# Edge sort of a four-layer graph network: the running table carried per four tiles instead of two

## The chip, the cores and the metric

The kernel runs on one core of a Trainium2 chip. Five engines take part: PE (TensorE, matmuls, which write the banks of PSUM), DVE (VectorE), ACT (ScalarE), POOL (GpSimd, which here mainly issues indirect DMAs, one row address per partition) and SP (which only issues DMAs). Each runs its own list of instructions in order and waits on counting semaphores that the others raise. The metric is the device time of one execution in microseconds (us), lower is better.

## What is computed

Four message-passing layers over 3125 nodes and 103125 edges (100000 random ones and a self-loop each), all with 256 features. Each layer has a segment sum over one end of the edges:

```python
_o = jnp.argsort(dst, stable=True)
src = src[_o]; dst = dst[_o]
...
h = layernorm_relu(x)
x = x + _L0_gnn_ref(h, edge_index, edge_attr_18, ...)               # softmax and sums by src
x = x + _L1_gnn_ref(layernorm_relu(x), edge_attr_64, edge_weight, ...)  # by dst
x = x + _L2_gnn_ref(..., src, dst, edge_type_8)                     # by dst
x = x + _L3_gnn_ref(..., src, dst, ...)                             # by dst
```

The kernel first writes the edges' records (attributes and a few words) into two arrays in HBM, one ordered by `src` and one by `dst`, so that the layers find the edges of a node block next to each other. The change is in this counting sort alone, in the two passes that scatter the records.

## The kernel before

`sort_all` (from line 152) does the sort. A tile is 128 edges, one per partition; there are 808 tiles. A key is split into `hi` (one of 25 node blocks) and `lo` (the place in the block). The position of an edge in the order is a start for its key, plus the number of edges with the same key in earlier tiles, plus the number of them ahead of it in its own tile.

- The **running table** (25 x 128, one entry for each key) holds the start plus what earlier tiles added. It is accumulated in PSUM bank `TABLE` by one matmul per tile, one-hot `hot_hi` by one-hot `hot_lo` (line 700), and copied by ACT into the SBUF tile `table` (line 604), which has two buffers.
- The **lookup** (line 705) multiplies the turned one-hots `hot_hi_t` with `table`, in fp32, into bank 2 or 3 (`c % 2`); DVE then picks the column by a product with `hot_lo` and a sum, which gives `base` (line 649). Two lookup banks are used in turn: the lookup of tile c waits on `row_used` for tile c-2's base.
- The **rank** (line 641) compares an edge's key with the keys of the tile, laid out along the free axis in bank 4 or 5 by `keys` (line 684), and sums the matches under the mask `earlier`.
- `positions` (line 631) adds base and rank for two tiles; POOL waits for it (`pos_ready`) and issues two indirect DMAs, one per tile, each of 128 record rows (line 564).

Tiles go in **steps** of G = 8, 101 of them per pass: first `scatter(keys_of[0], ...)` with `FirstPass` beside it (by `src`), then `scatter(keys_of[1], ...)` with `SecondPass` (by `dst`). A hardware loop holds `ROUND` = 4 steps; the order inside a step is written out by hand for each engine. DVE: ranks of tiles 0-3; bases 0, 1; one-hots of the next step (lines 340, 342); base 2, positions of the first pair; base 3, positions of the second pair; ranks of tiles 4-7; bases 4, 5; base 6, positions of the third pair; base 7, positions of the fourth; then what runs beside (in the first pass the one-hots for the next histogram). PE, for each pair d = 0 to 3 of the step: wait for `table_ready`, two table matmuls, two lookups; behind pair 1 it turns the first half of the next step's one-hots (line 672), behind pair 2 it turns the second half and lays out the first keys, behind pair 3 it lays out the second keys and does the histogram matmuls. ACT, for each pair: wait for `table_moved` and `looked_up`, copy the table; keys, turned one-hots (line 583) and the record's words (line 591) lie between. Records and `pos_i` have four buffers (`ROUND`), the one-hots, `base` and `rank` two.

Of the kernel before, what the change touches and what calls it, by code (L numbers as in the profile page):

```python
# [6 lines left out]
BF16 = mybir.dt.bfloat16  # L7
# [5 lines left out]
P = 128  # L13
# [12 lines left out]
PAIRS = G // 2  # L26
BUFS, BUFS2 = 4, 6
# [124 lines left out]
def sort_all(nc, C, A, x, by_src, by_dst, projected, kv0, q0):  # L152
# [48 lines left out]
    with phase(nc, "sort") as ph:  # L201
# [29 lines left out]
        junk = ph.sbuf("junk", [P, G, 3 * P], BF16)  # L231
        earlier = ph.sbuf("earlier", [P, 2, P], BF16)
# [42 lines left out]
        with ph.block() as block:  # L275
# [34 lines left out]
            def _(dve):  # L310
                dve.tensor_copy(ps[:, IOTA, 0:P], C.iota[:])
                dve.tensor_scalar(ident_hi[:], C.ident_b[:], float(BN), None, ALU.mult)
                dve.memset(earlier[:, 0, :], 1.0)
                dve.tensor_copy(earlier[:, 1, :], C.lower[:])
# [196 lines left out]
        def scatter(K, attr_dram, words, beside):  # L511
# [22 lines left out]
            with ph.block() as block:  # L534
# [36 lines left out]
                def _(act):  # L571
# [27 lines left out]
                    def body(j, b, ahead, tail):  # L599
                        n = at(j, b)  # L600
                        for d in range(PAIRS):
                            act.wait_ge(table_moved, n(PAIRS, d + 1))
                            act.wait_ge(looked_up, n(G, 2 * d))
                            act.copy(table[0:NB, (d + 1) % 2, :], ps[0:NB, TABLE, 0:P]).then_inc(table_ready, 1)  # L604
                            if ahead and d == 0:
                                if not opening(j, b, 1):
                                    act.wait_ge(pos_ready, n(PAIRS, 0))
                                keys(*ahead)
                            if ahead and d in (1, 2):
                                turn(*ahead, d - 1)  # L610
                            beside.scalar(act, j, b, d, tail)
# [6 lines left out]
                def _(dve):  # L618
# [14 lines left out]
                    def body(j, b, ahead, tail):  # L633
                        n, u = at(j, b), b % 2
                        for h in range(2):
                            dve.wait_ge(keys_ready, n(2, h + 1))
                            for c in range(4 * h, 4 * h + 4):

                                first, mates = (0, P) if c % 2 else (1, 0)
                                end = P * (c % 4) + P  # L640
                                last = dve.scalar_tensor_tensor(out=junk[:, c, 0:P + mates].rearrange("p (t e) -> p t e", e=P),  # L641
                                                                in0=ps[:, 4 + h, end - P - mates:end].rearrange("p (t e) -> p t e", e=P),
                                                                scalar=key_cur[:, u, c:c + 1], in1=earlier[:, first:2, :],
                                                                op0=ALU.is_equal, op1=ALU.mult, accum_out=rank[:, u, c:c + 1])
                            last.then_inc(ranked, 1)
                            for c in range(4 * h, 4 * h + 4):
                                dve.wait_ge(looked_up, n(G, c + 1))

                                dve.scalar_tensor_tensor(out=junk[:, c, 2 * P:3 * P], in0=ps[:, 2 + c % 2, 0:P], scalar=1.0,  # L649
# [11 lines left out]
                def _(pe):  # L661
# [2420 lines left out]
```

## Time and profile before

| | |
|---|---|
| time, median of 3 runs | 10085.68 us (10085.18 to 10108.67) |
| span of the profiled execution, first to last instruction | 9823.2 us |
| time that lies outside the span | 10085.7 - 9823.2 = 262.5 us |
| first scatter pass, first to last scatter | 267.9 to 1592.1 us, 1324.2 us |
| second scatter pass | 1620.6 to 2913.6 us, 1293.0 us |
| POOL busy in the first pass / DVE / PE | 784.5 / 799.9 / 762.9 us of 1329 |

The profile is one execution. It gives busy times per engine and line, what ended the idle time ahead of an instruction (the releaser), and a timeline. A releaser is found from the semaphores: "<-DVE sort_pos_i L631" is a wait that this line's end released; "<-remote" means that the semaphore rose just before, but no instruction's recorded end lies near that moment; "<-issue" means that no semaphore rose then. The ends of matmuls are modelled. All times below are from this execution's span, and the 262.5 us outside it are taken as unchanged.

### The profile page before, as it was taken

What the parts mean: (1) busy time and instruction counts of PE and PEld (TensorE: products, weight loads), DVE (VectorE), ACT (ScalarE), POOL (GpSimd) and SP (SyncE); (2) the same over time, 40 slices, a digit from 0 to 9 for tenths busy, and PEclk for the clock granted to TensorE, in tenths of its full rate; (3) what the DMA queues carried; (4) which work ended last, traced back from release to release, by engine and by line L of the source; (5) the groups of instructions that cost most, each with busy time, mean ns of one, the idle gap of its engine ahead of it and who ended that gap; (6) DMA issues with size and microseconds to landing.
All of it is one profiled execution on the core that took longest, in us unless ns stands there. A gap on an engine that the chain in (4) does not pass through costs nothing. (4 is left out here: it accounts for less than half of the span.)

```text
span 9823.2 us, 140985 instructions
## 1 busy us (share of the span) xinstructions
PE 6503.9 (66%) x32549; PEld 4804.2 (49%) x32550; DVE 5122.6 (52%) x15163; ACT 3750.0 (38%) x11176; POOL 5197.7 (53%) x5192
## 2 busy tenths in 40 slices
PE   8555555666657777777588888879644445566664
PEld 7445544554444555555366666656433324344443
DVE  6556655555545555555587777841122223344445
ACT  3212212222225555555266666734100001566663
POOL 0555655665655545455166666620466663566664
PEclk9776666666668988899799999989766667677776
DMA  7301102111114444344265565632333333333333
GB/s 221 92 13 14 13 13 61 27 26 27 26 27 110 107 104 107 98 108 103 91 172 159 157 161 156 166 102 69 84 89 89 92 90 70 84 90 89 89 89 75
DMA packets 1039015, 873.73 MB, mean 89 GB/s; under 512 B 746842, under 2 KB 855410, under 8 KB 1038360
## 3 DMA queue, kind: packets, MB, share of 16 engines
q0 software_dynamic: 259600, 655.15, 25.1%
q1 hardware_dynamic: 723939, 158.04, 8.3%
q10 hardware_dynamic: 54948, 54.63, 1.7%
q8 instruction: 196, 3.21, 0.1%
q14 instruction: 332, 2.71, 0.1%
HBM read 733.27 MB, written 134.17 MB: 88 GB/s over the span
## 5 line engine op out<-in xcount | busy, mean ns | idle before, releaser
L1164 POOL DMA_INDIRECT edges_kv<-kv,edges_rec x1712 | 1832.2, 1070 | 1432.6 <-issue 713.7
L1274 PE MATMUL banks<-edges_kv,edges_hot 128*128 128x288 f32 (+2 forms) x5136 | 1715.8, 489 | 757.7 <-DVE edges_kv L1549 621.1
L1274 PEld LDWEIGHTS banks<-edges_kv,edges_hot 128*128 128x128 f32 x5136 | 1158.9, 236 | 1138.0 <-ACT edges_pair_sums L1426 337.2
L564 POOL DMA_INDIRECT by_src_records<-sort_by_src_rec,sort_pos_i x808 | 784.5, 971 | 774.2 <-issue 483.2
L705 PE MATMUL banks<-sort_table,sort_hot_hi_t 128*128 128x128 f32 x3232 | 880.6, 413 | 423.9 <-DVE sort_junk L649 244.2
L1722 POOL DMA_INDIRECT edges_rows<-rel,edges_rec x856 | 811.5, 948 | 583.2 <-DMA edges_rec<-by_dst_records 326.3
L1164 POOL DMA_INDIRECT edges_kv<-feat,edges_rec x856 | 826.3, 965 | 526.1 <-issue 331.7
L564 POOL DMA_INDIRECT by_dst_records<-sort_by_dst_rec,sort_pos_i x808 | 784.6, 971 | 536.9 <-DVE sort_pos_i L631 302.2
L1738 PE MATMUL banks<-edges_rows,edges_hot 128*128 128x256 f32 x1712 | 604.2, 500 | 694.9 <-issue 417.8
L649 DVE SCALAR_TENSOR_TENSOR sort_junk<-banks,sort_hot_lo 128x128 bf16<-128x128 f32 x1616 | 438.5, 286 | 1055.8 <-remote 755.5
L705 PEld LDWEIGHTS banks<-sort_table,sort_hot_hi_t 128*128 128x128 f32 x3232 | 687.9, 291 | 508.2 <-DVE sort_junk L649 289.9
L1738 PEld LDWEIGHTS banks<-edges_rows,edges_hot 128*128 128x128 f32 x1712 | 416.4, 251 | 883.1 <-issue 583.1
L1391 ACT ACTIVATE edges_off<-columns,edges_column 128x128 bf16<-128x128 f32 x2568 | 784.5, 390 | 0.0
L583 ACT COPY sort_hot_hi_t<-banks 25x512 f32<-25x512 f32 x404 | 232.4, 575 | 1404.2 <-remote 780.0
L1776 DVE TENSOR_TENSOR agg<-banks,agg 128x256 f32 x428 | 181.0, 423 | 928.4 <-DMA tables_far<-far 606.1
L1363 ACT ACTIVATE edges_apart<-banks,minus_p 128x512 bf16<-128x512 f32 x642 | 431.5, 691 | 571.8 <-DMA sort_feat<-in_edge_attr_dram 311.7
L700 PE MATMUL banks<-sort_hot_lo,sort_hot_hi 128*128 128x128 bf16 x1616 | 299.9, 282 | 488.1 <-ACT sort_table L604 482.2
L641 DVE SCALAR_TENSOR_TENSOR sort_junk<-banks,sort_key_cur,sort_earlier 128x128 bf16<-128x128 f32 x1616 | 576.7, 413 | 5.8 <-PE banks L684 5.8
L1567 DVE TENSOR_TENSOR edges_kv<-banks,edges_kv 128x256 f32<-128x256 f32 x428 | 179.5, 420 | 687.7 <-PE banks L1234 393.6
L1234 PE MATMUL banks<-x,edges_hot_t 128*128 x1712 | 494.8, 414 | 58.3 <-issue 42.2
L1549 DVE TENSOR_TENSOR edges_kv<-edges_kv 128x1024 f32<-128x1024 f32 x428 | 519.9, 1215 | 3.4 <-ACT edges_kv L1408 3.4
L1582 DVE TENSOR_TENSOR edges_kv<-banks,edges_kv 128x256 f32<-128x256 f32 (+1 forms) x856 | 445.9, 552 | 137.5 <-remote 53.7
(440 smaller groups left out, 12977.2 us busy)
## 6 DMA issues: line engine op xcount, KB each, us to landing
edges_kv<-kv,edges_rec POOLq DMA_INDIRECT x1712
sort_feat<-in_edge_attr_dram SPq DMA_DIRECT2D x100, 256.0 KB
rel<-tables_stage SPq DMA_DIRECT2D x100, 252.0 KB
by_dst_records<-by_dst_blank ACTq DMA_DIRECT2D x1, 17120.0 KB
edges_rec<-by_dst_records SPq DMA_DIRECT2D x26, 640.0 KB
edges_rows<-rel,edges_rec POOLq DMA_INDIRECT x856
edges_kv<-feat,edges_rec POOLq DMA_INDIRECT x856
by_src_records<-sort_by_src_rec,sort_pos_i POOLq DMA_INDIRECT x808
```

Of the source, the lines that this page charges most:

```text
L564: pool.indirect_dma_start(O.rec, bass.IndirectOffsetOnAxis(ap=pos_i[:, b, c:c + 1], axis=0), rec[:, b, c, :], None).then_inc(scattered[b], 16)
L641: last = dve.scalar_tensor_tensor(out=junk[:, c, 0:P + mates].rearrange("p (t e) -> p t e", e=P), in0=ps[:, 4 + h, end - P - mates:end].re ...
L649: dve.scalar_tensor_tensor(out=junk[:, c, 2 * P:3 * P], in0=ps[:, 2 + c % 2, 0:P], scalar=1.0, in1=hot_lo[:, u, c, :], op0=ALU.mult, op1=A ...
L705: pe.matmul(ps[:, 2 + c % 2, 0:P], hot_hi_t[:, u, c, :], table[:, d % 2, :], start=True, stop=True).then_inc(looked_up, 1)
L1164: pool.indirect_dma_start(kv[:, r, c, 0:koff + DIM], None, tab, bass.IndirectOffsetOnAxis(ap=reci[:, b, c, idx:idx + 1], axis=0)).then_inc ...
L1234: last = pe.matmul(out[:, c, 2 * P - QW:2 * P], hot_t[:, b % 2, 2 * m + c, :], rows, start=(kind == 1), stop=(kind == 1 or c == 1), skip_g ...
L1274: last = pe.matmul(ps[:, 6 + m % 2, 0:OW], hot[:, b % 2, c, :], kv[:, b % BUFS, c, koff:koff + OW], start=(c % 2 == 0), stop=(kind != 1 an ...
L1391: last = act.activation(off[:, c, :], C.columns[:, c % 2, :], ACT.Abs, bias=column[:, b % 2, c:c + 1], scale=-1.0)
L1549: dve.tensor_tensor(v4, v4, bc(exps, dh), ALU.mult).then_inc(msg_done, 1)
L1582: dve.tensor_tensor(k2, by, k2, ALU.mult).then_inc(edges_used, 1)
L1722: pool.indirect_dma_start(rows[:, b, c, :], None, tab, bass.IndirectOffsetOnAxis(ap=reci[:, b, c, idx:idx + 1], axis=0)).then_inc(gathered ...
L1738: last = pe.matmul(sum_of(b, m), hot[:, b % SETS, c, :], rows[:, b, c, :], start=(c % 2 == 0), stop=(c % 2 == 1))
```

## The change

A step is now two groups of four tiles (`QUADS` = G // 4) instead of four pairs, in the table's hand-over between PE and ACT. Four table matmuls run in a row, then four lookups, with one copy of the table per four tiles. Since the table no longer tells of the tiles of the same four, a tile's rank counts those: tile c of four is compared with c + 1 tiles' keys (128, 256, 384, 512 columns), where it was 128 or 256. Positions and scatters stay in pairs. The work that lay behind pairs 1 and 2 or 2 and 3 on PE and ACT now lies behind the first and the second four.

```diff
-        junk = ph.sbuf("junk", [P, G, 3 * P], BF16)
-        earlier = ph.sbuf("earlier", [P, 2, P], BF16)
+        rank_junk = ph.sbuf("rank_junk", [P, QUADS, 10, P], BF16)
+        base_junk = ph.sbuf("base_junk", [P, G, P], BF16)
+        earlier = ph.sbuf("earlier", [P, 4, P], BF16)
...
-                dve.memset(earlier[:, 0, :], 1.0)
-                dve.tensor_copy(earlier[:, 1, :], C.lower[:])
+                dve.memset(earlier[:, 0:3, :], 1.0)
+                dve.tensor_copy(earlier[:, 3, :], C.lower[:])
...
-                        for d in range(PAIRS):
-                            act.wait_ge(table_moved, n(PAIRS, d + 1))
-                            act.wait_ge(looked_up, n(G, 2 * d))
-                            act.copy(table[0:NB, (d + 1) % 2, :], ps[0:NB, TABLE, 0:P]).then_inc(table_ready, 1)
-                            if ahead and d == 0:
+                        for q in range(QUADS):
+                            act.wait_ge(table_moved, n(QUADS, q + 1))
+                            act.wait_ge(looked_up, n(G, 4 * q))
+                            act.copy(table[0:NB, (q + 1) % 2, :], ps[0:NB, TABLE, 0:P]).then_inc(table_ready, 1)
+                            if ahead and q == 0:
...
-                            if ahead and d in (1, 2):
-                                turn(*ahead, d - 1)
-                            beside.scalar(act, j, b, d, tail)
+                            if ahead:
+                                turn(*ahead, q)
+                            beside.scalar(act, j, b, q, tail)
...
-                                first, mates = (0, P) if c % 2 else (1, 0)
-                                end = P * (c % 4) + P
...
+                                tiles = c % 4 + 1
+                                first = tiles * (tiles - 1) // 2
+                                last = dve.scalar_tensor_tensor(out=rank_junk[:, h, first:first + tiles, :],
+                                                                in0=ps[:, 4 + h, 0:tiles * P].rearrange("p (t e) -> p t e", e=P),
+                                                                scalar=key_cur[:, u, c:c + 1], in1=earlier[:, 4 - tiles:4, :],
...
-                        for d in range(PAIRS):
-                            pe.wait_ge(table_ready, n(PAIRS, d + 1))
-                            beside.tensor_table(pe, j, b, d, tail)
-                            for c in (2 * d, 2 * d + 1):
+                        for q in range(QUADS):
+                            quad = range(4 * q, 4 * q + 4)
+                            pe.wait_ge(table_ready, n(QUADS, q + 1))
+                            for c in quad:
                                 last = pe.matmul(ps[:, TABLE, 0:P], hot_hi[:, u, c, :], hot_lo[:, u, c, :],
                                                  start=False, stop=False, skip_group_check=True)
                             last.then_inc(table_moved, 1)
-                            for c in (2 * d, 2 * d + 1):
+                            for c in quad:
                                 pe.wait_ge(row_used[c % 2], n(4, c // 2))
-                                pe.matmul(ps[:, 2 + c % 2, 0:P], hot_hi_t[:, u, c, :], table[:, d % 2, :],
+                                pe.matmul(ps[:, 2 + c % 2, 0:P], hot_hi_t[:, u, c, :], table[:, q, :],
                                           start=True, stop=True).then_inc(looked_up, 1)
-                            if ahead and d in (1, 2):
-                                turn(*ahead, d - 1)
-                            if ahead and d in (2, 3):
-                                keys(*ahead, d - 2)
-                            beside.tensor(pe, j, b, d, tail)
+                            if ahead:
+                                turn(*ahead, q)
+                                keys(*ahead, q)
+                            beside.tensor(pe, j, b, q, tail)
```

In `FirstPass` and `SecondPass` the hooks follow: what hung on pair 3 hangs on the second four, what hung on pairs 0 and 1 on the first four, and the projection's matmuls (line 879), which stood behind pair 2, stand behind the second four.

PE in the middle of a step of the first pass, before: turning the first half (L672), the table and the lookups of tiles 4 and 5 (L700, L705), turning the second half.

```order
L672 MATMUL banks<-ident_b,sort_hot_hi 128x128 [waits sort_by_src_turned_copied,sort_by_src_hot_ready]
L672 MATMUL banks<-ident_b,sort_hot_hi 128x128 x3
L697 REGISTER_ALU
L700 MATMUL banks<-sort_hot_lo,sort_hot_hi 128x128 [waits sort_by_src_table_ready]
L700 MATMUL banks<-sort_hot_lo,sort_hot_hi 128x128
L705 MATMUL banks<-sort_table,sort_hot_hi_t 128x128 [waits sort_by_src_row_used0]
L705 MATMUL banks<-sort_table,sort_hot_hi_t 128x128 [waits sort_by_src_row_used1]
L670 REGISTER_ALU [waits sort_by_src_hot_ready]
L672 MATMUL banks<-ident_b,sort_hot_hi 128x128 [waits sort_by_src_turned_copied]
L672 MATMUL banks<-ident_b,sort_hot_hi 128x128 x3
```

The same place after (L674 turns, L686 lays out keys, L702 is the table, L707 the lookups of tiles 4, 5, 6, 7):

```order
L674 MATMUL banks<-ident_b,sort_hot_hi 128x128 [waits sort_by_src_turned_copied,sort_by_src_hot_ready]
L674 MATMUL banks<-ident_b,sort_hot_hi 128x128 x3
L680 REGISTER_ALU
L686 MATMUL banks<-sort_ident_hi,sort_halves 128x128 [waits sort_by_src_ranked,sort_by_src_seg_ready]
...
L702 MATMUL banks<-sort_hot_lo,sort_hot_hi 128x128 [waits sort_by_src_table_ready]
L702 MATMUL banks<-sort_hot_lo,sort_hot_hi 128x128 x3
L706 REGISTER_ALU
L707 MATMUL banks<-sort_table,sort_hot_hi_t 128x128 [waits sort_by_src_row_used0]
L707 MATMUL banks<-sort_table,sort_hot_hi_t 128x128 [waits sort_by_src_row_used1]
```

The eight key matmuls and all four table matmuls of tiles 4 to 7 now stand ahead of the lookups of tiles 4 and 5; the second turning and the first keys, which stood ahead of the lookups of tiles 6 and 7, do not any more.

DVE at the start of a step of the first pass, before:

```order
L641 SCALAR_TENSOR_TENSOR sort_junk,sort_rank<-banks,sort_key_cur,sort_earlier 128x128 [waits sort_by_src_keys_ready]
L641 SCALAR_TENSOR_TENSOR sort_junk,sort_rank<-banks,sort_key_cur,sort_earlier 128x256
L641 SCALAR_TENSOR_TENSOR sort_junk,sort_rank<-banks,sort_key_cur,sort_earlier 128x128
L641 SCALAR_TENSOR_TENSOR sort_junk,sort_rank<-banks,sort_key_cur,sort_earlier 128x256
L647 REGISTER_ALU
L649 SCALAR_TENSOR_TENSOR sort_junk,sort_base<-banks,sort_hot_lo 128x128 [waits sort_by_src_looked_up]
```

And after:

```order
L643 SCALAR_TENSOR_TENSOR sort_rank_junk,sort_rank<-banks,sort_key_cur,sort_earlier 128x128 [waits sort_by_src_keys_ready]
L643 SCALAR_TENSOR_TENSOR sort_rank_junk,sort_rank<-banks,sort_key_cur,sort_earlier 128x256
L643 SCALAR_TENSOR_TENSOR sort_rank_junk,sort_rank<-banks,sort_key_cur,sort_earlier 128x384
L643 SCALAR_TENSOR_TENSOR sort_rank_junk,sort_rank<-banks,sort_key_cur,sort_earlier 128x512
L649 REGISTER_ALU
L651 SCALAR_TENSOR_TENSOR sort_base_junk,sort_base<-banks,sort_hot_lo 128x128 [waits sort_by_src_looked_up]
```

Nothing moves on DVE; the third and fourth rank of a half grow by 256 columns each.

## Rows read from the trace of the kernel before

**Rows 1.** The page: span, and busy time of each engine in it.

```profile
span 9823.2 us, 140985 instructions
...
PE 6503.9 (66%) x32549; PEld 4804.2 (49%) x32550; DVE 5122.6 (52%) x15163; ACT 3750.0 (38%) x11176; POOL 5197.7 (53%) x5192
```

**Rows 2.** Busy time and mean clock in the two scatter passes, windows view.

```profile
core 0: us, PE busy (x) PEld busy (x) DVE busy (x) ACT busy (x) POOL busy (x), PEclk, DMA share, GB/s
266.00:1595.00 1329.00, 762.94 (x5618) 650.46 (x5615) 799.86 (x4021) 274.41 (x1199) 784.50 (x808) 0.68 0.14 27
1620.00:2916.00 1296.00, 811.22 (x4952) 641.39 (x4950) 700.57 (x3985) 308.39 (x1473) 784.56 (x808) 0.65 0.12 26
```

**Rows 3.** Line 564, the scatters: duration min/median/max in ns, first and last start.

```profile
L564 POOL DMA_INDIRECT by_src_records<-sort_by_src_rec,sort_pos_i x808: 966/972/1168, 267.9 to 1592.1; - x162
L564 POOL DMA_INDIRECT by_dst_records<-sort_by_dst_rec,sort_pos_i x808: 966/972/988, 1620.6 to 2913.6; - x162
```

**Rows 4.** Waits of 300 to 1600 us: total us, times, longest.

```profile
DVE sort_junk L649 <- remote: 384.3, 116, 4.9
ACT sort_table L604 <- remote: 315.5, 92, 8.9
...
POOL by_src_records L564 <- DVE sort_pos_i L631: 284.8, 98, 4.8
```

**Rows 5.** Timeline of one step of the first pass: start, us, engine, work, [idle before <-releaser].

```profile
1500.30 0.29 DVE L649 SCALAR_TENSOR_TENSOR sort_junk<-banks,sort_hot_lo 128x128 bf16<-128x128 f32 x1 [4.55 <-remote]
...
1501.48 0.97 POOL L564 DMA_INDIRECT by_src_records<-sort_by_src_rec,sort_pos_i  x1 [2.42 <-DVE sort_pos_i L631]
...
1502.76 0.97 POOL L564 DMA_INDIRECT by_src_records<-sort_by_src_rec,sort_pos_i  x1 [0.30 <-issue]
...
1505.91 0.15 DVE L631 TENSOR_TENSOR sort_pos_i<-sort_base,sort_rank 128x2 int32<-128x2 f32 x1
...
1506.45 1.17 PE L705 MATMUL banks<-sort_table,sort_hot_hi_t 128*128 128x128 f32 x4
...
1506.88 0.97 POOL L564 DMA_INDIRECT by_src_records<-sort_by_src_rec,sort_pos_i  x1 [0.60 <-issue]
...
1507.41 0.63 PE L672 MATMUL banks<-ident_b,sort_hot_hi 128*128 128x128 bf16 x4
...
1507.86 0.29 DVE L649 SCALAR_TENSOR_TENSOR sort_junk<-banks,sort_hot_lo 128x128 bf16<-128x128 f32 x1
...
1508.90 0.90 PE L705 MATMUL banks<-sort_table,sort_hot_hi_t 128*128 128x128 f32 x4
...
1510.05 0.57 ACT L583 COPY sort_hot_hi_t<-banks 25x512 f32<-25x512 f32 x1 [2.84 <-remote]
...
1510.71 0.97 POOL L564 DMA_INDIRECT by_src_records<-sort_by_src_rec,sort_pos_i  x1 [0.31 <-issue]
1513.03 0.29 DVE L649 SCALAR_TENSOR_TENSOR sort_junk<-banks,sort_hot_lo 128x128 bf16<-128x128 f32 x1 [4.67 <-remote]
1513.06 0.26 ACT L604 COPY sort_table<-banks 25x128 f32<-25x128 f32 x1 [2.44 <-remote]
...
1514.22 0.97 POOL L564 DMA_INDIRECT by_src_records<-sort_by_src_rec,sort_pos_i  x1 [2.54 <-DVE sort_pos_i L631]
```

**Rows 6.** Line 641 by shape, both passes: busy us, mean ns | idle before.

```profile
L641 DVE SCALAR_TENSOR_TENSOR sort_junk<-banks,sort_key_cur,sort_earlier 128x256 bf16<-128x256 f32 x806 | 385.8, 479 | 0.0
L641 DVE SCALAR_TENSOR_TENSOR sort_junk<-banks,sort_key_cur,sort_earlier 128x128 bf16<-128x128 f32 x806 | 279.2, 346 | 2.9 <-PE banks L684 2.9
```

**Rows 7.** Timeline of a step of the second pass, same columns.

```profile
2500.55 0.29 DVE L649 SCALAR_TENSOR_TENSOR sort_junk<-banks,sort_hot_lo 128x128 bf16<-128x128 f32 x1 [2.56 <-PE banks L705]
...
2502.19 0.29 DVE L649 SCALAR_TENSOR_TENSOR sort_junk<-banks,sort_hot_lo 128x128 bf16<-128x128 f32 x1 [1.34 <-PE banks L705]
...
2507.31 0.16 DVE L631 TENSOR_TENSOR sort_pos_i<-sort_base,sort_rank 128x2 int32<-128x2 f32 x1
...
2508.48 0.97 POOL L564 DMA_INDIRECT by_dst_records<-sort_by_dst_rec,sort_pos_i  x1 [0.30 <-issue]
```

More of the change, by code:

```diff
@@ L26 @@
 PAIRS = G // 2
+QUADS = G // 4
 BUFS, BUFS2 = 4, 6
@@ L647, in body @@
                                 dve.wait_ge(looked_up, n(G, c + 1))
-                                dve.scalar_tensor_tensor(out=junk[:, c, 2 * P:3 * P], in0=ps[:, 2 + c % 2, 0:P], scalar=1.0,
+                                dve.scalar_tensor_tensor(out=base_junk[:, c, :], in0=ps[:, 2 + c % 2, 0:P], scalar=1.0,
                                                          in1=hot_lo[:, u, c, :], op0=ALU.mult, op1=ALU.mult,
@@ L749, in count, with tensor @@
                 return last
-            @staticmethod
-            def tensor_table(pe, j, b, d, tail):
-                pass
             @classmethod
-            def tensor(cls, pe, j, b, d, tail):
-                if d == PAIRS - 1 and not opening(j, b, 1):
+            def tensor(cls, pe, j, b, q, tail):
+                if q == QUADS - 1 and not opening(j, b, 1):
                     pe.wait_ge(next_ready, at(j, b)(2, 0))
@@ L772, in scalar @@
             @staticmethod
-            def scalar(act, j, b, d, tail):
+            def scalar(act, j, b, q, tail):
                 pass
@@ L862, in tensor_table, with tensor @@
             @staticmethod
-            def tensor_table(pe, j, b, d, tail):
-                pass
-            @staticmethod
-            def tensor(pe, j, b, d, tail):
+            def tensor(pe, j, b, q, tail):
                 if tail or b != 2:
                     return
-                if d == 0:
+                if q == 0:
                     pe.wait_ge(cur_ready, j + 1)
@@ L875, in tensor @@
                     last.then_inc(cur_turned, 1)
-                if d == 2:
+                if q == 1:
                     pe.wait_ge(cur_copied, j + 1)
@@ L890, in scalar @@
             @staticmethod
-            def scalar(act, j, b, d, tail):
+            def scalar(act, j, b, q, tail):
                 if tail:
                     return
-                if b == 0 and d == 3:
+                if b == 0 and q == 1:
                     act.wait_ge(moments_ready, j * 3 + 3)
                     act.activation(root[:, 1:2], root[:, 0:1], ACT.Sqrt).then_inc(root_done, 1)
-                if b == 1 and d == 3:
+                if b == 1 and q == 1:
                     act.wait_ge(shift_ready, j * 2 + 2)
@@ L900, in scalar @@
                                    bias=shift[:], scale=root[:, 2:3]).then_inc(cur_ready, 1)
-                if b == 2 and d == 1:
+                if b == 2 and q == 0:
                     act.wait_ge(cur_turned, j + 1)
```

3 lines of the change are left out of this document (removed).

## The prediction, made before the changed kernel ran

> **What bounds the kernel now.** The page first: no engine fills the span, and the averages belong to many stages [rows 1]. The change touches only the two scatter passes, so I cut those out. In both, POOL, DVE and PE are each busy about 60% of the time [rows 2]: none is full, and the question is who waits for whom.
>
> POOL's own line shows the floor. A scatter takes 0.972 us and never much else [rows 3]; two in a row start 1.275 us apart (0.97 and an idle 0.30 that nothing ends) [rows 5]. A pass has 808, so its first and last would start 807 x 1.275 = 1029 us apart if POOL never waited. They start 1324.2 and 1293.0 us apart [rows 3]: POOL waits 295 and 264 us, 559 us together. That is all that this change could ever give. Nearly all of it is in one row: POOL waiting for the positions of line 631, 98 times in 101 steps, 2.9 us each [rows 4].
>
> Why are the positions late? One step answers it [rows 5]. DVE's base of tile 6 starts at 1500.30, and twelve and a half us later, at 1513.03, it is there again, after 4.67 us of idling on the lookup. But PE's record of that lookup (with tile 7's) is the one at 1508.90, which ends at 1509.80. ACT's table copy, which waits for an earlier matmul, starts within 0.03 us of DVE; both are put down to "remote", a semaphore that rose with nobody's end near it. So PE's results are there and are told late. When are they told? POOL's last scatter before it starves starts at 1510.71 and ends at 1511.68; the late signals come 1.35 us after that, and in the same way before 1500.30. Matmuls whose records end before about 1507.6 are seen at once (the lookups of tiles 4 and 5, 1506.45, are used at 1507.86); from the turning at 1507.41 on they are not. I read this as: while POOL has been issuing scatters for six or so us, PE's signals are held, and the bulk of them is let go when POOL has run dry. The cycle that follows is 8 scatters x 1.275 = 10.2, plus 1.35 until the held signals are seen, plus 1.19 from DVE's base at 1513.03 to POOL's start at 1514.22: 12.74 us, which is what a step takes (1293.0 / 101 = 12.8; the first pass, with some irregular stretches, 13.1).
>
> **The change part by part.**
>
> *Table hand-overs.* Two ACT copies of 0.26 us and two trips PE to ACT to PE fall out of each step. In the cycle above they are not late: at 1513 the copy and the base are released together, and POOL waits for the base. I value this at nothing; its cover is POOL's run of 10.2 us. What it is worth if that reading is wrong is a rival.
>
> The row shows two waits that end together, and gives no price for one signal more or less. The Trainium skill ("TensorE: Matmul & The Clock Gate", The cost: per-tile semaphore tail) says that increments by matmuls on completion serialize, at 26.3 ns each. By it the two increments fewer per step would save 202 x 2 x 0.026 = 11 us, against nothing in my sum.
>
> *Wider ranks.* 128 columns more cost 479 - 346 = 133 ns [rows 6]. Each half gains four times 128 columns, 0.53 us; a step 1.06 us, both passes 215 us of DVE. DVE in the first pass goes from 800 to 907 of 1329 us, still the smaller part, so it is not the total but the place that counts. In the first pass the first pair's positions start at 1505.91 and end at 1506.06; POOL's scatter for them starts at 1506.88, after 0.60 us of idling instead of 0.30 [rows 5]. From the end of positions to POOL's start always lie about 0.8 us (1514.22 has it too). So these positions are already 0.30 us late, nothing hides more, and the 0.53 us of the first half's ranks, which stand ahead of them, come on top of each step: 101 x 0.53 = 54 us. The second half's 0.53 us lies in front of base 4, while POOL works through four scatters (5.1 us from 1506.88); hidden. In the second pass the same positions end at 2507.47 for a scatter at 2508.48, 1.01 us; less the 0.82 it needs that leaves 0.19 us [rows 7]. That step holds the layer norm's statistics, as one in four does; there 0.34 us stick out, 25 x 0.34 = 9 us. The other steps have some 0.9 us more and hide it.
>
> *PE's order.* The lookups of tiles 4 and 5 now stand behind the first keys and two more table matmuls. From the two turnings and what lies between them to the next lookups [rows 5] I estimate 1.1 us for that; with the ranks' 0.53 they would start at about 1508.1 instead of 1506.45 and yield the first result near 1508.9. DVE asks for base 4 at 1507.86 + 1.06 = 1508.92. Just in time, if the signal is told at once: nothing. In return, nothing stands between lookups 5 and 6 any more; with the drain as the releaser that gives nothing either.
>
> *SBUF, DMAs:* the same scatters, loads and stores; no cost.
>
> Sum: 54 + 9 = 63 us on 10085.7, 10149 us. Bounds: below, the whole wait of POOL, -559; above, the restart of the second rival.
>
> **The rivals.**
>
> *Slower by a longer restart.* With the first result at 1508.9, lookup 4 falls 7.4 us into POOL's run that began at 1501.48, where the trace shows signals held. Then after the drain DVE must do base 4, PE lookup 6, DVE base 6, before positions can go. The second pass shows such a hop: base at 2500.55, the next but one base on the same bank at 2502.19, 1.64 us [rows 7]; unheld it would be nearer 1.2. If it hits each step of the first pass only: 101 x 1.64 + 63 = 229, 10315 us; both passes, less what the second already pays: up to +350. It decides from the point where lookup 4 ends later than six or so us into the run. I take 10330.
>
> *Faster: fewer signals ahead of the needed one.* Not all held signals wait for the drain: ACT's copy at 1510.05 was let go alone, 3 us before the rest [rows 5]. Before, three signals of PE (the turning, the keys, the table) stand ahead of lookup 6; now none does. If held signals leave one by one, lookup 6 takes the early slot, positions come up to 3 us sooner and POOL's 2.5 us gap closes. ACT's 315.5 us of table waits [rows 4], too, would halve. In half the steps of both passes: 0.5 x 202 x 2.5 = 252, less 63: -190, 9895 us; in a fifth of them -40. Against it: lookups 4 to 7 also come later.
>
> *No difference.* The first pass' irregular stretches (13.1 against 12.8 a step, 30 us) go while the ranks cost their 54, or DVE's late pair is absorbed in the wait behind it: within 30 us of before. This is also how it would look if the hand-over simply weren't where time goes and the ranks had cover that one step doesn't show.
>
> **How the numbers follow.** A measurement can tell about 0.3%, 30 us. Forecast (10149; by itself 10105 to 10200): 0.40, of which 0.07 lies inside 30 us. Longer restart: 0.17. No difference: 0.18. Faster: 0.25. So slower 0.33 + 0.17 = 0.50, same 0.25, faster 0.25. For the range I leave out the part of the faster case below 9950 (0.09) and of the restart case above 10350 (0.08): 9950 to 10350.
>
> **What would show it.** The ranks at 346, 479, about 612 and 745 ns. POOL's scatters still in runs of eight with one wait of about 2.5 us a step ahead of the third pair, and a second, of 0.8 us instead of 0.3, ahead of the first pair in the first pass; the passes at about 1378 and 1302 us from first to last scatter. A wait of 3.7 us or more in front of the third pair, with base 4 released together with ACT's table copy, is the longer restart. POOL runs longer than eight scatters, or table waits of ACT that vanish along with POOL's, are the faster case. It is wrong at its root if PE's signals are told at once in the new order: then POOL's floor, not the drain, would set the step.

## The result: 1.6 to 2.0% slower, and the profile after

The changed kernel took 10250.5 us (median of 4; 10245.3 to 10280.0), the kernel before 10085.4 (median of 4). Three of those four are the runs of the table above, from before the prediction; the one that was added is 10056.7 us. The medians give 1.0164, 165 us. The reported ratio is 1.0196, with a 95% interval of 1.0164 to 1.0228, which by its size goes with the added run (10250.5 / 10056.7 = 1.0193). So the loss is 165 to 197 us, its size rests on few runs of before, and the changed kernel was measured again further down. The forecast was 10149 us, slower by 63. The sign and the range held; the size was 2.6 to 3.1 times too small.

The time of the profiled execution is its span and 1.7 us (10246.5 against 10244.8), and so it is in every later run of both kernels. So nothing to speak of stands outside the span. By that rule the execution of [rows 1], with a span of 9823.2 us, took about 9825 us and was shorter than its neighbours; this is worked out, its own time is not on record. The two profiles differ by 421.6 us, of which some 256 belong to that one execution of before. A second trace of before, further down, is the one to compare with.

The scatters of the changed kernel, in the view of one line (duration min/median/max in ns, first and last start), which answer to [rows 3]:

```profile
L566 POOL DMA_INDIRECT by_src_records<-sort_by_src_rec,sort_pos_i x808: 964/970/1167, 266.6 to 1748.4; - x162
L566 POOL DMA_INDIRECT by_dst_records<-sort_by_dst_rec,sort_pos_i x808: 964/970/982, 1776.3 to 3236.3; - x162
```

A scatter costs what it did, 0.97 us. The passes take 1481.8 and 1460.0 us from first to last start, where 1378 and 1302 were forecast. The waits of 300 to 1700 us (total us, times, longest) answer to [rows 4]:

```profile
ACT sort_table L606 <- remote: 705.7, 95, 8.0
...
POOL by_src_records L566 <- DVE sort_pos_i L633: 457.4, 108, 5.0
DVE sort_base_junk L651 <- remote: 448.8, 95, 5.4
```

The wait for the positions is still about one a step, but it is longer: 457.4 us in 108 times, 4.2 us each, where it was 2.9. Where it stands is in the timeline of a step (start, us, engine, work, [idle before <-releaser]), which answers to [rows 5]:

```profile
1502.64 0.97 POOL L566 DMA_INDIRECT by_src_records<-sort_by_src_rec,sort_pos_i  x1 [4.83 <-DVE sort_pos_i L633]
...
1506.44 0.40 PE L702 MATMUL banks<-sort_hot_lo,sort_hot_hi 128*128 128x128 bf16 x4
...
1511.56 0.97 POOL L566 DMA_INDIRECT by_src_records<-sort_by_src_rec,sort_pos_i  x1 [0.30 <-issue]
1514.29 0.26 ACT L606 COPY sort_table<-banks 25x128 f32<-25x128 f32 x1 [7.86 <-remote]
1514.34 0.29 DVE L651 SCALAR_TENSOR_TENSOR sort_base_junk<-banks,sort_hot_lo 128x128 bf16<-128x128 f32 x1 [5.00 <-remote]
...
1514.55 0.29 DVE L651 SCALAR_TENSOR_TENSOR sort_base_junk<-banks,sort_hot_lo 128x128 bf16<-128x128 f32 x1
...
1514.76 0.36 DVE L342 TENSOR_TENSOR sort_hot_hi<-banks,sort_by_src_hi 128x200 bf16<-128x200 f32 x1
1515.04 1.22 DVE L344 TENSOR_TENSOR sort_hot_lo<-banks,sort_by_src_lo 128x1024 bf16<-128x1024 f32 x1
1516.17 0.28 DVE L651 SCALAR_TENSOR_TENSOR sort_base_junk<-banks,sort_hot_lo 128x128 bf16<-128x128 f32 x1
...
1516.38 0.16 DVE L633 TENSOR_TENSOR sort_pos_i<-sort_base,sort_rank 128x2 int32<-128x2 f32 x1
...
1517.36 0.97 POOL L566 DMA_INDIRECT by_src_records<-sort_by_src_rec,sort_pos_i  x1 [4.83 <-DVE sort_pos_i L633]
```

POOL's scatter at 1502.64 is the first of a step, and so the wait now stands ahead of the first pair, not the third. The eight scatters run to 1512.53. PE's table matmuls of 1506.44 end at 1506.84, but ACT's copy that waits for them starts at 1514.29. Then DVE does base 0, base 1, the two one-hot instructions of the next step (1514.76 to 1516.17, 1.41 us) and base 2, and only at 1516.38 the first positions. That is the restart: 1.8 us until the signals are told, 2.0 from there to the positions, 0.16 for them and 0.8 to POOL's start at 1517.36, 4.8 us, of which 0.30 stand between any two scatters. The cycle is 10.2 + 4.5 = 14.7 us, and the starts of every eighth scatter are 14.7 us apart (median, first pass; 14.6 in the second). In [rows 5] the same instructions stood outside the restart, and the cycle was 12.8.

### The profile page after: what moved, and what is told of

It reads as the page before. It is cut to its first block and busy times, and to the rows that moved or that the text cites. A ratio compares the mean times of both kernels' runs of the same rounds, so it can differ in the third digit from the quotient of the medians.

```text
span 10244.8 us, 139889 instructions
## 1 busy us (share of the span) xinstructions
PE 6397.7 (62%) x32549; PEld 4750.4 (46%) x32550; DVE 5365.0 (52%) x15163; ACT 3678.7 (36%) x10772; POOL 5181.8 (51%) x5192
## 5 line engine op out<-in xcount | busy, mean ns | idle before, releaser
L707 PE MATMUL banks<-sort_table,sort_hot_hi_t 128*128 128x128 f32 x3232 | 817.8, 395 | 1372.2 <-DVE sort_base_junk L651 1312.7
L707 PEld LDWEIGHTS banks<-sort_table,sort_hot_hi_t 128*128 128x128 f32 x3232 | 642.6, 277 | 1472.2 <-DVE sort_base_junk L651 1409.9
L651 DVE SCALAR_TENSOR_TENSOR sort_base_junk<-banks,sort_hot_lo 128x128 bf16<-128x128 f32 x1616 | 446.5, 288 | 1142.5 <-remote 994.6
L643 DVE SCALAR_TENSOR_TENSOR sort_rank_junk<-banks,sort_key_cur,sort_earlier 128x128 bf16<-128x128 f32 (+1 forms) x1616 | 792.8, 547 | 5.8 <-PE banks L686 5.8
L606 ACT COPY sort_table<-banks 25x128 f32<-25x128 f32 x404 | 103.1, 255 | 1470.7 <-remote 1325.9
```

The costliest lines, as they stand in the source:

```text
L643: last = dve.scalar_tensor_tensor(out=rank_junk[:, h, first:first + tiles, :], in0=ps[:, 4 + h, 0:tiles * P].rearrange("p (t e) -> p t e", ...
L651: dve.scalar_tensor_tensor(out=base_junk[:, c, :], in0=ps[:, 2 + c % 2, 0:P], scalar=1.0, in1=hot_lo[:, u, c, :], op0=ALU.mult, op1=ALU.mu ...
L707: pe.matmul(ps[:, 2 + c % 2, 0:P], hot_hi_t[:, u, c, :], table[:, q, :], start=True, stop=True).then_inc(looked_up, 1)
```

## The experiments

The kernels of a group below ran on the same chip, each group on another one. The groups fall into two kinds: in two of them the kernel before took about 10,070 us, as at first, in three about 8,290 us. I call the kinds A and B. Each of these five chips was used in one group only, so whether the kind belongs to the chip or to the time of the runs isn't shown. What the profiles show of the difference is under the last heading. Times are compared within a group.

### Before, again; and its rank widths, the one-hots and PE's order apart (kind B)

The kernel before, unchanged.

> The kernel before, unchanged, to have its time and trace from the same chip as the experiments. The changed kernel's time was its span + 1.7 us, while the profiled execution of before had a span of 9823.2 us against a median of 10085 us. Theory D (that execution was an unusually short one; the time is always span + about 2 us): the span here is about 10083 us, the two scatter passes take about 2880 us together (1424 and 1393 in scatters) instead of 2617, some 14.0 us a step instead of 12.8, and the changed kernel's real loss is 0.8 us a step. Rival F (a fixed part outside the span): span 9823 us again, time 262 us above it.

It took 8287.2 us, ratio 1.0002 (0.9992 to 1.0011) to its twin. The profiled execution took 8282.5 us with a span of 8280.8; rival F falls here, but theory D's numbers can't be tried where no signal comes late. The scatters:

```profile
L564 POOL DMA_INDIRECT by_src_records<-sort_by_src_rec,sort_pos_i x808: 965/969/1166, 266.4 to 1294.5; - x162
L564 POOL DMA_INDIRECT by_dst_records<-sort_by_dst_rec,sort_pos_i x808: 965/969/986, 1316.6 to 2344.0; - x162
```

1028.1 and 1027.4 us: the floor of 1029 us that the prediction worked out, with no waits above it. The same 0.97 us a scatter, the same program; and in the whole list of waits of this trace no row has "remote" as its releaser. Here is what POOL waits for between 300 and 1200 us:

```profile
POOL by_src_records L564 <- issue: 202.5, 663, 0.8
...
POOL by_src_records L564 <- DVE sort_pos_i L631: 13.4, 44, 0.3
```

These are the 0.30 us between two scatters (215.9 us in 707 times), whoever they are put down to. Now the wide ranks in the kernel before (shortened):

```
-  in0=ps[:, 4 + h, end - P - mates:end], in1=earlier[:, first:2, :]
+  in0=ps[:, 4 + h, 0:tiles * P],         in1=earlier[:, mask:mask + tiles, :]
   # tiles = c % 4 + 1; masks: zero for the earlier pair, then as before
```

> The kernel before with only the changed kernel's rank widths (128, 256, 384 and 512 columns, masks that are zero for the earlier pair, so the same results). The change's extra rank time is 2 x (133 + 266) = 0.8 us a step on DVE. Theory R (the late second pair of each four is the loss): ratio to before 1.010 to 1.016, 100 to 165 us, and a wait that grows by about 0.8 us a step. Theory C (the loss comes from where the eight scatters' row is cut and what DVE and ACT must redo before it starts again): ratio 0.999 to 1.006.

8296.3 us, ratio 1.0008 (0.9998 to 1.0017). Theory C had named 0.999 to 1.006, but on kind B POOL's issue covers everything, so it says only that the wider ranks have cover where nothing is told late. They are 1.06 us a step, as in the prediction, and not the 0.8 us of the expectation: the third and the fourth rank of a half grow by 133 + 133 ns each (613 and 746 ns against 346 and 479). In the changed kernel, the one-hots moved:

```
-  if c == 1 and ahead:      # the next step's one-hots, line 656
+  if c == 3 and ahead:
```

> The changed kernel with the next step's one-hots (two DVE instructions, 1.41 us) issued behind the positions of the second pair instead of behind base 1, so that they no longer stand between the first lookups and the first pair of positions. Theory C: the wait ahead of the first pair falls from 4.5 to about 3.1 us, a step takes 13.3 us instead of 14.7, and the time is 10250 - 202 x 1.4 = 9967 us (ratio to before 0.988). Theory R: the ranks are what is late, the time stays within 40 us of 10250 (ratio 1.012 to 1.020).

8426.9 us, 1.0173 (1.0156 to 1.0190): slower than either kernel is here. The passes took 1136.0 and 1040.3 us: the steps of the first are 11.2 us long. Neither expectation could be tried, since both were for kind A. I read the loss so: PE turns the one-hots, ACT copies them, PE looks up with them; each of these starts later by what the one-hots were put back, and the loop over the engines is then longer than 10.2 us. That reading is argued, no run splits it. And PE's order of before in the changed kernel:

```
-  if ahead:
-      turn(*ahead, q)
-      keys(*ahead, q)       # both behind each four lookups
+  if ahead and c in (3, 5): # inside the loop over the tiles, behind lookup c
+      turn(*ahead, c // 4)
+  if ahead and c in (5, 7):
+      keys(*ahead, c // 2 - 2)
```

> The changed kernel (table per four tiles, wide ranks) with the next step's turns and key copies standing between PE's lookups as in the kernel before: the turn of half 0 behind lookup 3, turn 1 and keys 0 behind lookup 5, keys 1 behind lookup 7, instead of behind each four. Theory P (PE's order alone made the loss: keys and turns stand ahead of lookups): the cut goes back to the third pair and the time to 10085 +- 30 us (ratio 1.000). Theory C says that order only shifts which signals are told late: between 10190 and 10300 us (ratio 1.010 to 1.021). Theory R: 10250 as well.

8302.3 us, 1.0016 (1.0006 to 1.0025), with POOL at its floor as above. It decides nothing, since the changed kernel wasn't beside it and no step has a cut.

### The changed kernel again, and lookups in one bank per four (kind A)

> The changed kernel, unchanged. In the last four runs the kernel before took 8288 us instead of 10085, its POOL ran one scatter per 1.273 us through both passes without a wait (10.18 us a step), and no engine waited for a signal without a releaser; so these runs lack what makes the steps 12.8 to 14.7 us long in the first traces. Theory C (the change only moves the place where signals that come late cut the row of eight; where none come late, POOL's issue covers everything): if the kernel before takes 8288 us again, ratio 0.999 to 1.004; if it takes about 10085 us, 1.016 again. Rival L (the changed kernel's own loop over DVE, ACT and PE, with four table moves behind each other and the one-hots ahead of the first pair, is longer than 10.18 us): ratio 1.008 to 1.017 at 8288 us, with a wait ahead of the first or third pair in each step of the first pass, as with the one-hots later (10.2 to 11.2 us a step).

This group had the kernel before at 10069.3 us, and the changed kernel at 10236.3: ratio 1.0151 (1.0102 to 1.0201), passes of 1475.5 and 1455.6 us. The first result repeats in sign and rough size. The second kernel (shortened):

```
-  pe.wait_ge(row_used[c % 2], n(4, c // 2))          # for each lookup
-  pe.matmul(ps[:, 2 + c % 2, 0:P], ...).then_inc(looked_up, 1)
+  # once per four: the bank's last readers of the step before
+  last = pe.matmul(ps[:, 2 + q, P * (c % 4):P * (c % 4) + P], ...)
+  ...
+  last.then_inc(looked_up, 1)                        # once per four
```

> The changed kernel with the four lookups of a four written into one bank's four quarters, told by one signal, and PE waiting once per four for the bank's last reader of the step before, instead of for each lookup's predecessor by two. Theory C where signals come late: fewer round trips behind the late signal, but lookups 4 to 7 can also run ahead of it: the cut stays ahead of the first pair, 0.3 to 0.8 us a step less than the changed kernel (60 to 160 us). Where none come late: nothing, within 0.3% of the changed kernel. Rival L: PE's lookups were in its loop, at 8288 us it is faster than the changed kernel by 0.5 to 1%.

10222.3 us, 14 us below the changed kernel, whose interval covers that; the passes, 1482.0 and 1483.4 us, are not shorter. Three fewer signals a four and no lookup that waits for its predecessor by two: it buys nothing that these runs can tell, and the wait stays ahead of the first pair in nearly every step. The 60 to 160 us that I expected did not come. The likely reason, from the step shown above, is that the first signal that DVE needs is already a held one, and the restart begins with it; no run tries this.

### PE's order, the one-hots and the changed kernel once more (kind B)

> The same kernel as in the run of e4 (the changed kernel with PE's turns and key copies between the lookups, as before). There the kernel before took 8288 us and nothing came late; the last call had the kernel before at 10069 us and the changed one at 1.015. If the kernel before takes about 10070 us in this call too: theory P (the change loses because its PE order sends the turns and keys ahead of nothing, so that the row of eight is cut ahead of the first pair instead of the third) expects a ratio of 0.996 to 1.004 and the wait back ahead of the third pair; theory R (wide ranks) and theory M (the table moved per four) expect 1.012 to 1.018 and the wait of 4.5 us ahead of the first pair. If the kernel before takes 8288 us: 1.0016 again, which decides nothing.

Kind B: 8301.5 us, 1.0013 (1.0003 to 1.0022), which decides nothing, as said.

> The same kernel as in the run of e3 (the changed kernel, the next step's two one-hots behind the second pair's positions). If the kernel before takes about 10070 us in this call: theory C (when signals come late, DVE's 1.41 us of one-hots stand in the restart between base 1 and base 2) expects the wait ahead of the first pair to fall from 4.5 to 3.1 us and a ratio of 0.985 to 0.995; rival L (the one-hots delay PE's turns for the next step, which is what cost 1.6% where nothing came late) expects 1.015 to 1.035, later turns giving back more than the restart gains. If the kernel before takes 8288 us: 1.017 again.

8417.4 us, 1.0149 (1.0132 to 1.0166). Here the changed kernel ran beside it:

> The changed kernel beside the two above. With the kernel before at about 10070 us: 1.015 again (10220 to 10255 us). With the kernel before at 8288 us, not yet measured: theory C expects 0.999 to 1.004, since the loss is then no property of the change but of late signals; rival L expects 1.008 to 1.017 and waits ahead of the first pair.

8300.8 us, ratio 1.0011 (1.0001 to 1.0020). **On kind B the change costs nothing in the passes**:

```profile
L566 POOL DMA_INDIRECT by_src_records<-sort_by_src_rec,sort_pos_i x808: 965/970/1167, 268.2 to 1296.5; - x162
L566 POOL DMA_INDIRECT by_dst_records<-sort_by_dst_rec,sort_pos_i x808: 965/970/987, 1318.8 to 2347.1; - x162
```

1028.3 and 1028.3 us, together 1.1 us above before's two passes on another chip of this kind. Rival L falls: the changed kernel's own loop fits below 10.2 us. And the one-hots' later place costs 117 us against it, as much as the passes grow (2173.3 against 2056.6 us).

### PE's order on kind A, and before's own trace there

> The same kernel as e4 and e4b, which both fell where the kernel before takes 8290 us. Where it takes about 10070 us, theory P (PE's order moves the cut) expects a ratio of 0.996 to 1.004 and the wait ahead of the third pair, 12.8 to 14 us a step; theories R (wide ranks) and M (the table moved per four) expect 1.012 to 1.018 and 4.5 us ahead of the first pair.

This group ran on a chip of kind A (before 10077.0 us). 10153.2 us, ratio 1.0082 (1.0055 to 1.0108): between the two expectations. The changed kernel had 1.0151 and 1.0196 on other chips of this kind, with intervals down to 1.0102. By that PE's order is something like half of the loss; the changed kernel didn't run on this chip, so the share is rough. Its passes:

```profile
L566 POOL DMA_INDIRECT by_src_records<-sort_by_src_rec,sort_pos_i x808: 963/969/1166, 265.8 to 1732.1; - x162
L566 POOL DMA_INDIRECT by_dst_records<-sort_by_dst_rec,sort_pos_i x808: 963/969/984, 1759.9 to 3142.7; - x162
```

1466.3 and 1382.8 us. And the kernel before, beside it:

> The kernel before beside it, for a trace from the same chip. Where its time is about 10070 us: theory D expects a span of 10060 to 10080 us, so that the first profiled execution (9823 us) was shorter than its normal runs, with 13.5 to 14.1 us a step in the two passes; rival F expects 9823 us of span again, and the difference to the time outside it.

10065.0 us, 0.9995 (0.9977 to 1.0013); span 10052.6, 7 us below what theory D named and 229 above rival F's. This is the trace of before that is to be compared:

```profile
L564 POOL DMA_INDIRECT by_src_records<-sort_by_src_rec,sort_pos_i x808: 963/970/1166, 267.0 to 1673.5; - x162
L564 POOL DMA_INDIRECT by_dst_records<-sort_by_dst_rec,sort_pos_i x808: 963/972/986, 1702.2 to 3055.7; - x162
```

1406.5 and 1353.4, together 2760 us. The changed kernel on kind A had 1475.5 + 1455.6 = 2931 (on another chip of the kind): 171 us more, and the median of that group is 167 us above its before. Outside the passes the two traces take 7302.1 and 7292.6 us. Nearly all of the loss is in the passes.

Why 1406.5 for a pass, and 1324.2 at another time? The kernel before has two lengths of step, and goes from one to the other. First POOL's waits in two stretches of 100 us of its first pass, 490 to 590 and 690 to 790 (total us, times, longest), the rows of each stretch behind the other:

```profile
ACT sort_hot_hi_t L583 <- remote: 39.8, 8, 5.8
...
POOL by_src_records L564 <- DVE sort_pos_i L631: 21.7, 8, 2.7
```

```profile
ACT sort_table L604 <- remote: 51.5, 7, 8.2
...
POOL by_src_records L564 <- DVE sort_pos_i L631: 32.5, 8, 4.9
```

2.7 us against 4.1 a time. The timelines show where each stands. A step of the first stretch, as in [rows 5], with ACT's copy of the turned one-hots and DVE's base of tile 4 told late and the wait ahead of the third pair:

```profile
532.16 0.58 ACT L583 COPY sort_hot_hi_t<-banks 25x512 f32<-25x512 f32 x1 [5.80 <-remote]
532.35 0.29 DVE L649 SCALAR_TENSOR_TENSOR sort_junk<-banks,sort_hot_lo 128x128 bf16<-128x128 f32 x1 [4.85 <-remote]
...
533.54 0.97 POOL L564 DMA_INDIRECT by_src_records<-sort_by_src_rec,sort_pos_i  x1 [2.71 <-DVE sort_pos_i L631]
```

And one of the second, with the table copy told late and the one-hots between the base and the positions, ahead of the first pair:

```profile
705.97 0.97 POOL L564 DMA_INDIRECT by_src_records<-sort_by_src_rec,sort_pos_i  x1 [4.39 <-DVE sort_pos_i L631]
...
717.64 0.26 ACT L604 COPY sort_table<-banks 25x128 f32<-25x128 f32 x1 [7.45 <-remote]
717.69 0.29 DVE L649 SCALAR_TENSOR_TENSOR sort_junk<-banks,sort_hot_lo 128x128 bf16<-128x128 f32 x1 [2.56 <-remote]
...
718.39 1.22 DVE L342 TENSOR_TENSOR sort_hot_lo<-banks,sort_by_src_lo 128x1024 bf16<-128x1024 f32 x1
...
720.71 0.96 POOL L564 DMA_INDIRECT by_src_records<-sort_by_src_rec,sort_pos_i  x1 [4.44 <-DVE sort_pos_i L631]
```

The second is the changed kernel's step, in the kernel before. I counted, from the starts of all scatters, the steps (of the last 100 of each pass) that have a gap of over 3.5 us ahead of the first pair (long) and those with one of over 1.8 us ahead of the third and less than 1 us ahead of the first (short); the rest are in between:

```
                          first pass    second pass   passes, us
                          long short    long short
before, first trace         21    63       0    99        2617
before, again (kind A)      53    36       0    99        2760
PE's old order (kind A)     85     2      41    37        2849
changed, again (kind A)     96     0      76    12        2931
changed, first trace        98     0      81     8        2942
```

The second and third row are from one chip; the others are from others of this kind. The time of a pass follows the share of long steps. The lengths keep to themselves: in the kernel before a first pass is cut into stretches of ten to thirteen steps which are nearly all long or nearly all short, and they change over at the stretches' borders. The borders are in the trace. In every pass of the kind A traces, behind the first scatter of each twelfth step (every third round of the loop), POOL stands still for 1.0 to 1.9 us, put down to no signal, eight times a pass; here is one in this trace:

```profile
603.58 0.97 POOL L564 DMA_INDIRECT by_src_records<-sort_by_src_rec,sort_pos_i  x1 [0.60 <-issue]
606.40 0.97 POOL L564 DMA_INDIRECT by_src_records<-sort_by_src_rec,sort_pos_i  x1 [1.85 <-issue]
```

The long steps begin behind this one. On kind B the passes in which POOL never waits have no such pause, but the first passes of the kernel with the one-hots later, where it waits in many steps, have it at the same eight places (1.76 to 1.86 us). So it is no mark of kind A. What makes it, and whether it is what tips the loop over, no run shows. A long step is 14.7 us and a short one 12.7 to 12.9. 172 long ones against 53 are 119 more, by 1.8 us: 214 us. Before's second pass has some longer gaps beside its short steps (mean 13.4, median 12.95, 45 us in 101 steps), which is the rough difference to the 171 measured.

### The wide ranks, once more (kind B)

What stayed open was the other half of the loss, 10153 against 10077 us.

> The kernel before with the changed kernel's rank widths alone. Where the kernel before takes about 10070 us its steps have two lengths, 12.8 us (cut ahead of the third pair) and 14.7 us (cut ahead of the first); the changed kernel has the long one in nearly all steps, and with PE's old order (10153 us) in about three quarters of them. Theory R (the wide ranks make the other half of the loss: positions later, so that fewer steps keep the short length): ratio 1.004 to 1.010, and more steps of 14.7 us. Theory M (moving the table per four makes it): 0.998 to 1.002, steps as in the kernel before. Where it takes 8290 us: 1.0008 again, which decides nothing.

Kind B, 8294.7 us, 1.0007 (0.9997 to 1.0017). It decides nothing. Whether the wide ranks or the table moved per four make the 76 us that PE's order doesn't give back **stays open**, and so does what putting the one-hots later would do on kind A: it would take 1.41 us out of the restart, and might cost what it cost on kind B. No version that beats the kernel before was found.

## Why the prediction came out as it did

**The floor: right.** 1029 us a pass from 807 x 1.275. Kind B shows 1028 with nothing told late. The bound "559 us" is what POOL loses in the first trace of before; in the second trace it is 702 us (2760 against twice 1029), so the bound was too low for the kernel's usual runs, with no effect on the forecast.

**That signals told late set the step: right, and seen from both sides.** Where no wait is put down to "remote" the change costs 0.1%; where some are it costs 1.5 to 2%. The kinds were met and not set, so this is a difference between groups of runs and not an experiment. The changed kernel's table copies wait 1309 us for late signals over the run (195 times, the second trace of it), before's 557 (138 times), and they are let go together with the lookup that DVE waits for (1514.29 and 1514.34): half as many hand-overs save nothing, as the prediction valued them. The two increments fewer a step, for which the rule of the Trainium skill that the prediction named ("TensorE: Matmul & The Clock Gate", The cost: per-tile semaphore tail) would give 11 us, don't show: on kind B the changed passes are 1.1 us longer, with POOL's issue as their cover, and taking six more increments a step out (the bank per four, kind A) didn't shorten the passes. That is no test of the rule's 26.3 ns, only of what it is worth here.

**That the cut stays ahead of the third pair: wrong.** This is the step that failed. The prediction put the start of the holding "from six or so us on" into POOL's run, read off one step. In the changed kernel PE's table matmuls end 4.2 us into the run (1506.84 against 1502.64) and are told 7.4 us later. The term that it gave "just in time: nothing", PE's order, is about half of the loss: with the old order the passes give back 82 of the 171 us (2931 to 2849, on different chips). The other 89 us are not split between the wide ranks and the table moved per four. The mechanism of the longer restart was among the rivals, at 0.17 and 10330 us, but at another place: it had the third pair wait for a round trip over lookup 6, and missed that the row could be cut ahead of the first pair, where DVE's one-hots, 1.41 us, lie inside the restart. That the sign and the range held was therefore luck: the 63 us were added up for a wait ahead of the third pair, which 98 of the last 100 steps of the first pass no longer have, and the range reached 10250 us only by way of that rival.

**The trace had it.** The first pass was called "12.8, with some irregular stretches, 13.1". Those stretches are 21 steps with the wait ahead of the first pair, and the longest of 4.8 us in [rows 4] beside a mean of 2.9 is one of them. They were the second state of the loop, 14.6 us against 12.8, and the question to ask of the change was which of the two it favours: 1.9 us a step, in up to 202 steps, 380 us at most.

**The ranks: the size right, the place not shown.** 346, 480, 613 and 746 ns against the forecast 346, 479, 612 and 745:

```profile
L643 DVE SCALAR_TENSOR_TENSOR sort_rank_junk<-banks,sort_key_cur,sort_earlier 128x512 bf16<-128x512 f32 x189 | 141.0, 746 | 0.0
L643 DVE SCALAR_TENSOR_TENSOR sort_rank_junk<-banks,sort_key_cur,sort_earlier 128x384 bf16<-128x384 f32 x189 | 115.9, 613 | 0.0
```

But the positions that were to be late by 0.53 us a step are now those that the restart waits for, and their ranks (1507.37 on, for the step that restarts at 1514.3) are long done. Their direct price has no place in a long step; whether they help to make steps long is the question that stays open. In the kernel before, on kind B, the same widths cost nothing (1.0008, 1.0007).

**That 262.5 us lie outside the span: wrong.** In the later runs the time is 1.7 us above the span (10054.3 and 10052.6 us for before on kind A, 8282.5 and 8280.8 on B). The forecast's own base, the median, was not hurt by it, but the view of the pass was: the normal first pass has 53 long steps of 100, not 21, and a reader of that trace sees a kernel that is better than it is.

## What to carry to other kernels

Where a loop shows one wait a turn, look at the turns that don't fit, by their starts, before costing a change: a loop over several engines can have two lengths of step that each last for many turns, and an edit can be paid for by which of them it favours. Ask what would have to be redone if the row were cut at another place, and whether large independent work (here 1.41 us of one-hots) stands between the first signal and the first result. Compare the span of the profiled execution with the times before taking its stretches as the kernel's normal ones; and have a second trace of the kernel before where its loop is irregular.

## What the runs showed of the hardware

The same program, with the same 0.97 us a scatter, took about 10,070 us in the groups of one kind and 8,290 us in those of the other, 18% less. The two traces of the kernel before differ by 1772 us: 704 in the scatter passes, where kind A has the late signals, and 1067 in the rest of the program, which has such waits too on kind A but was not looked into. Two more things differ. The mean granted clock of TensorE was 0.68 and 0.65 in the two passes on kind A and 0.80 and 0.77 on kind B (PE is busy for a smaller part of the time on A, 760.5 of 1408 us against 639.9 of 1029 in the first pass). And the profiler recorded fewer than half as many semaphore updates for the same program, 55,198 against 121,031, those of all engines. So on kind A a wait can be put down to "remote" because the right record is missing; that the waiters start late is in their own rows. It also leaves open whether the recording itself takes part in the lateness.

On kind A the first such rows, over the whole of the kernel before:

```profile
DVE sort_junk L649 <- remote: 782.8, 250, 6.6
ACT sort_hot_hi_t L583 <- remote: 775.2, 142, 8.4
```

On kind B there is none. In the passes on kind A most of them end after POOL has run dry: of DVE's waits for a lookup that are put down to "remote", 183 of 211 in the changed kernel (first trace) and 151 of 250 in the kernel before (second trace) end 1.3 to 1.9 us after the end of a scatter, 17 and 63 while a scatter is running. That POOL's issuing holds the signals is the reading that fits most of them, but no run took the scatters away to show it. The Trainium skill ("Perfetto Trace Analysis", Tensor Engine Instruction) says that the end of a matmul's row is an estimate and that the signal's way to the other engines is not in the profile. So a small gap between the row's end and the waiter's start says little. The trace of the changed kernel on kind B shows how small it is, 0.03 us at one and the same place of a step:

```profile
703.31 0.40 PE L702 MATMUL banks<-sort_hot_lo,sort_hot_hi 128*128 128x128 bf16 x4
...
703.74 0.26 ACT L606 COPY sort_table<-banks 25x128 f32<-25x128 f32 x1 [0.44 <-PE banks L702]
```

On kind A it is 7.4 us, from 1506.84 to 1514.29. What makes the kinds differ, no run here shows.
